# Deformable bottleneck plus quantised bottleneck: the first pair's offset convolution is issued ahead of the second pair's group sums

## The reference, cut to what matters

```python
out = conv(x, w1)                                   # 1x1, 256 -> 64 channels
out = relu(group_norm(out, gn1_scale, gn1_bias))    # 32 groups of 2 channels
om = conv(out, w_off, pad=1) + b_off                # 3x3, 64 -> 27: offsets and mask
mask = sigmoid(om[:, 18:])
sampled = bilinear_sample(out, py, px) * mask       # 9 taps at shifted positions
out = einsum('bckhw,ock->bohw', sampled, w2)
out = relu(group_norm(out, gn2_scale, gn2_bias))
out = group_norm(conv(out, w3), gn3_scale, gn3_bias)
x = relu(out + x)
```

## Time and profile before

| | us |
|---|---|
| median of 3 runs | 90.41 |
| the runs | 90.43, 89.57, 90.41 |
| the profiled execution's own time | 90.49 |
| its span, first to last instruction | 88.7 |
| PE busy in it | 75.2 (85%) |
| DVE busy | 65.4 (74%) |
| ACT busy | 50.1 (56%) |

### The profile page before, as it was taken

How to read it: one execution, slowest core, us unless ns; L and a number is a source line. 1 busy time by engine, 2 the same in 40 slices (tenths; PEclk the granted TensorE clock), 3 DMA queues, 4 the chain that set the end, 5 groups by cost and what they waited for, 6 DMA issues and landing times.

```text
span 88.7 us, 2177 instructions
## 1 busy us (share of the span) xinstructions
PE 75.2 (85%) x893; PEld 51.6 (58%) x893; DVE 65.4 (74%) x176; ACT 50.1 (56%) x89; POOL 5.0 (6%) x10
## 2 busy tenths in 40 slices
PE   5988999996899898999999999899589887779600
PEld 1333666475698797888988897345233374555400
DVE  0424539999999789999897725899896784967850
ACT  4203165679974999996868003906672254732660
POOL 7600110000000000000003100000000000000000
PEclk9999999999999999999999999999999999999995
DMA  1999800000000000000000000000000000000076
GB/s 30 326 317 313 346 12 0 7 0 0 0 7 0 0 7 0 4 11 0 0 7 0 0 0 7 0 0 0 0 0 0 0 0 0 0 7 4 5 258 211
DMA packets 3290, 4.17 MB, mean 47 GB/s; under 512 B 272, under 2 KB 2704, under 8 KB 3280
## 3 DMA queue, kind: packets, MB, share of 16 engines
q1 hardware_dynamic: 3008, 3.76, 13.0%
q10 hardware_dynamic: 272, 0.26, 0.9%
HBM read 2.98 MB, written 1.05 MB: 45 GB/s over the span
## 4 chain that ended last, share of the span: by engine, by line
PE 43%; DVE 31%; ACT 10%; DMA 6%; issue 4%; SPq 2%; DVEq 0%; ACTq 0%
PE acc L492 15%; PE slot L479 10%; DVE g_rows L926 9%; DMA x_sb<-x 6%; PE acc L624 4%; DVE g_cols L1028 3%; PE acc L603 3%; PE slot L407 3%; ACT g_cols L728 2%; PE slot L528 2%; ACT g_cols L826 2%; DVE g_cols L1074 2%; ACT pad L785 2%; PE slot L564 2%; DVE g_cols L1166 2%
## 5 line engine op out<-in xcount | busy, mean ns | idle before, releaser
L926 DVE TENSOR_TENSOR g_rows<-hats 128x2304 f32<-128x2304 f32 (+1 forms) x12 | 20.6, 1753 | 0.1
L728 ACT ACTIVATE g_cols<-slot 128x768 f32<-128x768 f32 x24 | 17.8, 829 | 3.7 <-PE slot L479 3.7
L492 PE MATMUL acc<-g_cols,v_sb 128*64 128x128 f32 x288 | 17.7, 276 | 0.0
L492 PEld LDWEIGHTS acc<-g_cols,v_sb 128*64 128x64 f32 x288 | 15.5, 137 | 1.1 <-issue 0.3
L370 PE MATMUL slot<-zeros 128*128 128x512 bf16 x54 | 15.0, 412 | 1.0 <-DVE zeros L845 1.0
L479 PE MATMUL slot<-consts_sb,g_rows 64*128 64x64 f32 x288 | 11.8, 226 | 2.1 <-DVE g_rows L926 1.7
L479 PEld LDWEIGHTS slot<-consts_sb,g_rows 64*128 64x128 f32 x288 | 10.3, 140 | 3.9 <-DVE g_rows L926 2.6
L370 PEld LDWEIGHTS slot<-zeros 128*128 128x128 bf16 x54 | 5.5, 109 | 6.9 <-issue 2.1
L785 ACT ACTIVATE pad<-g_cols 64x256 bf16<-64x256 int8 x8 | 3.3, 417 | 4.9 <-DVE g_cols L1074 4.8
L857 DVE BATCH_NORM_STATS2 stats<-acc 128x6 f32<-128x256 f32 x4 | 1.7, 430 | 4.1 <-PE acc L382 2.5
L407 PE MATMUL slot<-feat,woff_sb 128*64 128x256 f32 x36 | 4.7, 385 | 0.0
(11 more groups left out here) (141 smaller groups left out, 118.1 us busy)
## 6 DMA issues: line engine op xcount, KB each, us to landing
x_sb<-x SPq DMA_DIRECT2D x3, 256.0 KB, 4.5
out<-g_cols SPq DMA_DIRECT2D x3, 256.0 KB, 2.3
wq_sb<-wq SPq DMA_DIRECT2D x1, 484.5 KB, 6.3
woff_sb<-woff SPq DMA_DIRECT2D x1, 288.0 KB, 5.6
w_sb<-w SPq DMA_DIRECT2D x1, 288.0 KB, 5.5
x_sb<-x ACTq DMA_DIRECT2D x1, 256.0 KB, 2.9
w_sb<-w SPq DMA_DIRECT2D x1, 256.0 KB, 6.4
out<-g_cols SPq DMA_DIRECT2D x2, 128.0 KB, 1.8
```

Of the source, the lines that this page charges most:

```text
L492: mm = nc.tensor.matmul(acc[b2][rows(h), at:at + P], v_sb[:, B2 * h + b2, q, k, :], g_cols[t][h][:, NQ * k + q, :], start=(k == 0 and q == ...
L728: nc.scalar.activation(dst.rearrange("p k (r n) -> p k r n", r=HALVES), src.rearrange("p r (k n) -> p k r n", k=per), ACT.Copy).then_inc(g ...
L926: tt(g_rows[i % 3][:, taps], hats[:, t, h, 1, taps].unsqueeze(3).to_broadcast(shape), hats[:, t, h, 0, taps].unsqueeze(2).to_broadcast(sha ...
```

## The change

On TensorE alone the order of the stretch 2 to 3 is rewritten. The three fillers of `idle(IDLE[2], spare)` are gone. After `conv1(1)` come the waits for `woff_in` and for the first pair's `feat_ready`, then step 0 of the first pair's offset convolution, then `pair_sums(2, 1)`, then steps 1 to 4. Of the second pair, step 0 runs, then `om_turn(0)`, then steps 1 to 4. The wait for `w2_in` stands ahead of `make_v` as it did. Every other engine's program is the same.

```diff
             pair_sums(1, 0)
             conv1(1)
-            idle(IDLE[2], spare)
-            pair_sums(2, 1)
-
...
-            pe.wait_ge(woff_in, 16)
-            for b2 in range(B2):
-                pe.wait_ge(feat_ready, b2 + 1)
-                for s in range(TAPS_A):
-                    mm = om_step(b2, s)
-                    if b2 == 1 and s == 1:
-                        pe.wait_ge(consts_in, 16)
-                        om_turn(0)
-                mm.then_inc(om_done, 1)
...
+            pe.wait_ge(woff_in, 16)
+            pe.wait_ge(feat_ready, 1)
+            for s in range(TAPS_A):
+                mm = om_step(0, s)
+                if s == 0:
+                    pair_sums(2, 1)
+            mm.then_inc(om_done, 1)
+            pe.wait_ge(feat_ready, 2)
+            for s in range(TAPS_A):
+                mm = om_step(1, s)
+                if s == 0:
+                    pe.wait_ge(consts_in, 16)
+                    om_turn(0)
+            mm.then_inc(om_done, 1)
+            pe.wait_ge(w2_in, 16)
             for i in range(4):
                 make_v(i)
             om_turn(1)
```

More of the change, by code:

```diff
@@ L420, in om_turn @@
                 mm.then_inc(omt_done, 1)
-            pe.wait_ge(woff_in, 16)
-            for b2 in range(B2):
-                pe.wait_ge(feat_ready, b2 + 1)
-                for s in range(TAPS_A):
-                    mm = om_step(b2, s)
-                    if b2 == 1 and s == 1:
-                        pe.wait_ge(consts_in, 16)
-                        om_turn(0)
-                mm.then_inc(om_done, 1)
             v_banks = [small[0], small[1], acc[0], acc[1]]
-            pe.wait_ge(w2_in, 16)
             def make_v(i):
```

## The result

In the first measurement the kernel became slower, by about 1%. The changed kernel took 91.13 us at the median (91.07 to 92.25, 4 runs), the kernel before 90.42 (89.57 to 90.44, 4 runs): ratio 1.0129, 95% interval 1.0086 to 1.0171. Further down, medians are over all executions of a label, while the ratios leave out disturbed ones (mostly those with a mean granted clock of 0.977 or less, some 2 us longer), except that the 92.25 of the first measurement (0.975; without it the means give 1.010) and two of the six executions of the last run are still in. Forecast were 90.4 us, no change, and a range up to 90.8.

What follows compares the result with a forecast made beforehand. The prediction took TensorE's path through the V matmuls to ACT as the bound, priced at make_v: the turn starts 0.44 earlier, a 0.43 step moves behind it, net -0.03, so 90.49 becomes 90.46, or 90.4 at the median; range 89.6 to 90.8.

Steps and rivals of the forecast that it cites:

- The bound: Ahead of the sampling, TensorE's V matmuls feeding ACT bind; DVE's gain only lengthens its wait, 0.9 to about 1.2 us.
- DVE is the bound: Rival: turn 2 or the third product's first turns hang on DVE, so the 0.32 goes through: 90.1 us; chance 15%.
- Steps, drain, turn: TensorE, sums (9.48) to make_v (15.09): 0.43 us a step, sums 0.31 behind the step's last start, turn 0.44 earlier.
- The release: On TensorE, a waiting step or turn starts 0.06 us after its operand is ready; both at 0.15 add 0.18.
- lower bound of -0.15: At make_v: the start moves by -0.15 to +0.15 us, -0.03 taken; without drain it is 0.09 less.
- The sums stand behind a late step 0: Rival: on TensorE, pair_sums waits behind woff and feat, woff landing late or releases slow: 90.6 to 90.7 us; chance 12%.
- price rule: At make_v: from a step 0 at 8.93 on, each tenth of delay costs a tenth.
- The clock: Rival: without the fillers TensorE's clock falls; 9 to 15 us takes 2 to 3 us more, about 93; chance 3%.
- The range: Whole kernel: 89.6 to 90.8 us, set by the 0.86 us spread of the three runs of before.

Runs made afterwards that it cites:

- the last run: The kernel before with the first channel half of the second pair's convolution ahead of the first pair's sums, and 6 fillers ahead of conv1(0): 91.21 us, ratio 1.0106.
- the changed kernel's second profile: The changed kernel measured again with no edit: 90.85 us, ratio 1.0029 to the kernel before; its profiled execution took 90.48 us.
- the step without the wait: The changed kernel with step 0 of the first pair replaced by four instructions on x ahead of the sums, waits for woff and feat behind: 90.53 us, ratio 0.9984.

## Why the prediction was wrong

**The bound.** Right. All profiles whose clock held that far show 9.69 to 9.70 us from the V matmuls to the sampling, whatever else was moved, and DVE's earlier offsets went into its wait for ACT (0.9 to 1.2), as forecast. In the changed kernel the first offsets come 0.33 earlier against the V matmuls than before (15.68 - 12.67 against 15.09 - 12.41), and the sampling didn't follow them. That DVE is the bound, as the chain says, is refuted by this.

**Steps, drain, turn.** Right within 0.06. Forecast from the sums to the V matmuls: 15.09 - 9.48 = 5.61; measured 5.63 in four profiles of that order. The step with its drain holds the sums back by 0.58 (9.47 to 10.05), forecast 0.58 (8.90 to 9.48). The 0.31 that the prediction took from rows 4 for the drain is in it: the Trainium skill's rule (TensorEngine Tiling (Array Packing), Key Properties) and the measurement agree.

**The release.** A size was off: I took 0.06 from feat to the waiting step, and it is 0.14 to 0.15 (9.33 to 9.47, and 9.06 to 9.20 with 6 fillers). That is 0.08, and it was inside the bounds. DVE's offsets to the waiting turn, also taken as 0.06, are 0.11 (13.14 to 13.25). The lower bound of -0.15 doesn't follow from the terms beside it: -0.03 less 0.09 is -0.12. Nothing hangs on it.

**The step that failed** is "feat of the first pair is ready at 8.27 + 0.57 = 8.84 ... so step 0 starts at 8.90". In the changed kernel's profile feat was ready at 9.33, so step 0 started at 9.47 and the sums at 10.05, not at 9.48. I took two times of one execution, feat at 8.84 and mv at 9.30, as fixed, and bounded only the two release latencies around them. They are ends of two chains with different sources: feat hangs on the first pair's convolution, whose length goes with the clock's rise (1.26, 1.48, 1.98 us in three profiles of the two kernels); the second pair's mv hangs on that or on x's landing, whichever is later. The profile of before happened to have an early feat and a late x, the case in which the new order loses least. Its own row said so: the convolution of the second pair waited 0.38 for x at 7.95. That the changed kernel's second profile comes out at 90.48 is luck of the same kind, not a confirmation. In the kernel before, feat may come up to about 9.75 at no cost, since it is first used at 9.89; that slack of some 0.9 us was visible, and I spent it without asking what it had been absorbing.

**The rivals.** "The sums stand behind a late step 0" is what happened, with its price rule right (each tenth costs a tenth: 10.05 - 9.48 = 0.57 later than forecast, V matmuls 0.59 to 0.62 later), but I let only woff make it late and gave it 12%. The clock was looked for in the wrong place: as a fall right behind the removed fillers, which no profile shows, instead of in its rise during the first convolution, which the slow pace of the first seven fillers already pointed to. And the granted clock of 1.00 that I held against this rival couldn't speak: the row for 1 to 4 us reads 1.00 too, over these slow fillers. Its price of about 93 us is near what the four executions that lost the clock without the fillers took, 92.0 to 93.0.

**The range.** I took the spread of the three runs as noise on both kernels alike. Part of it is probably the same mechanism (the run of 89.57 has no profile, so this isn't shown), and the change made the kernel hang on it more: 0.61 against 0.26 us between 8 and 6 fillers.

## What to carry to other kernels

Before a wait is put ahead of other work on an engine, follow both operands back to their sources, and price the wait at the spread of these sources, not at the gap that one profile shows between them. Slack of a microsecond on a chain that starts at the kernel's first instructions is absorbing something: look at what varies there, such as matmuls at the lower clock or the landing of loads. Filling an idle engine with work that is ready anyway cost nothing here; filling it with work that has to be waited for cost up to 0.7 us by the profiles' intervals.

## What the runs showed of the hardware

The moment at which TensorE's clock rises differs from execution to execution of one kernel, and with it the first convolution: 1.26 and 1.98 us for the same eight instructions in two profiles of the changed kernel. It is read from the pace of the matmuls; the granted clock in the rows stays at 1.00 there. The changed kernel's executions differ with it by 0.6 us (90.4 to 91.0 or 91.1 within one comparison), as much as the whole effect looked for. The Trainium skill (TensorE: Matmul & The Clock Gate, Part 1) says that the point of the rise varies from run to run; the rows agree. Together with the one execution of 92.25 us it can account for ratios of 1.0129 with 4 executions and 1.0029 with 12 for the same two kernels; that nothing else took part isn't shown.

TensorE's clock can also fall in the middle of the kernel, long behind the rise. In two profiles (the kernel before without the three fillers, and the step without the wait) the granted clock is 0.50, the lower level, from 25 to 27 us. TensorE was busy for 0.21 and 0.29 of the microsecond from 21 to 22 and for 0.89 of the one from 23 to 24; the profile of the kernel before has 0.22 and 0.89 there and keeps 1.00. What decides it, no run here shows.
